# Products whose results nobody reads, in TensorE's pauses of a four-stage transformer pass

## The reference

```python
x = x + attn_a(layernorm(x), w_qkv, b_qkv)      # local: 16 heads of 16, softmax over groups of 32 tokens
x = x + ffn(layernorm(x), cn_*, gc_*, adaptive_range)
x = x + attn_b(layernorm(x), Wq, Wk, Wv, Wo, lambda_*, subln_g)
x = x + ffn(layernorm(x), cn_*, gc_*, adaptive_range)

# ffn: a gate of four small layers (256, 128, 64, 1), used three times
for _ in range(3):
    tf = sigmoid(gelu(gelu(gelu(out @ w1 + b1) @ w2 + b2) @ w3 + b3) @ w4 + b4)
    coupling = 0.1 + adaptive_range * (0.7 * gf + 0.3 * tf - 0.5) * 2.0
    out = out + coupling * twist(out)
# attn_b: differential attention over all 1024 tokens: 32 score maps with heads of 8,
# w = softmax(even map) - lam * softmax(odd map), values of width 16, RMS norm per head, then Wo
```

## Time and profile before

| | |
|---|---|
| Time, median of 3 runs | 8156.35 us (8153.01 to 8161.66) |
| Profiled execution, own time | 8150.33 us |
| Its span, first to last instruction | 8145.2 us |
| Busy: PE, DVE, ACT, POOL | 7508.5, 6885.6, 6208.0, 3537.0 us (92, 85, 76, 43%) |
| Mean granted TensorE clock | 0.959 |
| DMA | 297.66 MB, 37 GB/s in the mean |

### The profile page before, as it was taken

The page is one execution under the profiler, slowest core; times in us unless marked ns, Lnnn a source line. Parts: engine busy times, 40 slices in busy tenths (PEclk is TensorE's granted clock), DMA queues, the critical chain, the costliest instruction groups (busy, mean ns, idle before and its releaser), DMA issues. The chain is left out here.

```text
span 8145.2 us, 163210 instructions
## 1 busy us (share of the span) xinstructions
PE 7508.5 (92%) x64448; PEld 2698.0 (33%) x64448; DVE 6885.6 (85%) x8962; ACT 6208.0 (76%) x11230; POOL 3537.0 (43%) x4675
## 2 busy tenths in 40 slices
PE   6899988999889998899988999889998899989999
PEld 4322343223432234322343223432234322343223
DVE  5799768997689976899768997689976999669996
ACT  3599755997569975699756997569975699656996
POOL 4256233652336623355233662345513456134661
PEclk9899988999899998999998999999999999999999
DMA  0121101221012200121001210022200222002210
GB/s 31 48 47 44 29 12 49 47 47 24 12 54 44 47 23 12 55 47 44 21 12 56 47 44 22 9 58 46 48 21 7 62 43 48 23 4 63 45 44 25
DMA packets 591392, 297.66 MB, mean 37 GB/s; under 512 B 477238, under 2 KB 515638, under 8 KB 590582
## 3 DMA queue, kind: packets, MB, share of 16 engines
q1 hardware_dynamic: 590588, 286.82, 14.5%
HBM read 123.83 MB, written 67.37 MB: 23 GB/s over the span
## 5 line engine op out<-in xcount | busy, mean ns | idle before, releaser
L1459 DVE TENSOR_REDUCE mall<-ps 128x1 f32<-128x1024 f32 x4096 | 4662.3, 1212 | 80.7 <-PE ps L1396 80.0
L1544 ACT ACTIVATE work<-ps 128x512 f32<-128x512 f32 x8192 | 4335.7, 598 | 177.9 <-PE ps L1411 33.6
L1425 PE MATMUL ps<-work,vbuf 128*32 128x256 f32 x32768 | 2620.7, 392 | 58.6 <-ACT hh L1550 58.6
L1396 PE MATMUL ps<-kop,qop 48*128 48x512 bf16 x8192 | 2521.0, 386 | 46.8 <-DVE mall L1459 25.9
L1411 PE MATMUL ps<-qop,kop 51*128 51x512 bf16 x8192 | 2511.7, 384 | 24.6 <-DMA qop<-mT 13.7
L1425 PEld LDWEIGHTS ps<-work,vbuf 128*32 128x32 f32 x32768 | 654.0, 108 | 1727.8 <-issue 1001.7
L1411 PEld LDWEIGHTS ps<-qop,kop 51*128 51x128 bf16 x8192 | 512.9, 93 | 1783.4 <-ACT work L1544 1657.5
L1484 POOL TENSOR_TENSOR mall<-mall 128x16 f32<-128x16 f32 x512 | 113.9, 222 | 1772.8 <-DVE mall L1459 1752.8
L251 POOL TENSOR_TENSOR rstd<-rstd,nhalf 128x8 f32<-128x8 f32 x64 | 109.3, 1708 | 1637.8 <-DVE rstd L245 1637.8
L443 POOL TENSOR_TENSOR hh<-work,hmask 128x1024 f32<-128x1024 f32 x256 | 521.2, 2064 | 452.2 <-POOLq L1648 331.1
L1510 POOL TENSOR_TENSOR work<-work,none 128x16 f32<-128x16 f32 x224 | 650.6, 2904 | 18.2
(11 more groups left out here) (179 smaller groups left out, 8666.0 us busy)
## 6 DMA issues: line engine op xcount, KB each, us to landing
qop<-scratch SPq DMA_DIRECT2D x512, 64.0 KB
scratch<-work SPq DMA_DIRECT2D x32, 768.0 KB, 4.2
scratch<-hh SPq DMA_DIRECT2D x32, 768.0 KB, 3.6
kop<-scratch SPq DMA_DIRECT2D x256, 96.0 KB
vbuf<-in_x SPq DMA_DIRECT2D x9, 2048.0 KB, 8.3
qop<-scratch SPq DMA_DIRECT2D x512, 32.0 KB
kop<-scratch SPq DMA_DIRECT2D x256, 64.0 KB
out<-x SPq DMA_DIRECT2D x64, 256.0 KB, 2.1
```

The costliest lines, as they stand in the source:

```text
L1396: pe.matmul(ps[:, b + n, :], qop[r:r + KQ, s, i, t * P:(t + 1) * P], kop[r:r + KQ, s, i, half(n)], start=True, stop=True).then_inc(s_ms, 1)
L1425: mm = pe.matmul(ps[VW * i:VW * (i + 1), OB, cols], vp[:, b, t, (G * gl + i) // 2, :], prob[:, u % PS, i, cols], start=t == 0 and part == ...
L1459: v.tensor_reduce(mall[:, m // CUT % 2, to, col:col + 1], ps[:, b:b + NB, :].rearrange("p b n -> p (b n)"), AX.X, ALU.max).then_inc(s_mr, 1)
L1544: act.activation(prob[:, u % PS, hl, :], ps[:, EB[slot % len(EB)], :], ACT.Exp, scale=scale).then_inc(s_ex, 1)
```

## The change

A helper `busy` is added, which issues products of the identity with the first half of w1 into a named PSUM bank. Each has 128 rows, 128 columns of weights and 256 moving columns in f32. Nobody reads them, they wait for nothing, and they signal nothing. It is called at six places of TensorE's list, and no other engine's list is touched:

```diff
+        def busy(pe, bank, count):
+            for _ in range(count):
+                pe.matmul(ps[:, bank, 0:D], ident[:, :], w1[:, 0, :], start=True, stop=True)
...
                 def _(pe):                                   # layernorm: n2, n3, n4
+                    busy(pe, 7, 4)
                     for t in range(4 * N0, TT):
                         norm_turned(pe, t, s_h, s_tp)
...
+                    busy(pe, 7, 5)                           # local_attention
                     for t in range(TT + 2):
                         if t < TT:
                             scores(t)
...
                     layers(2, A)                             # ffn: f1, f2
+                    busy(pe, 5, 3)
                     layers(1, Z)
...
+                    busy(pe, 5, 4)
                     layers(2, Z)
...
                     project_pe(pe)                           # diff_attention
+                    busy(pe, 2, 6)
                     for e in CLOCK:
                         if value_tile(e) is not None:
                             project_values(pe, value_tile(e))
```

## The result

The changed kernel takes 8166.27 us (median of 20 runs, 8154.54 to 8170.11), the kernel before 8149.72 (20 runs beside them, 8131.49 to 8177.26). The ratio is 1.0019, with a 95% interval of 1.0011 to 1.0027: slower by 0.2%, where 0.2% faster was forecast. The profiled execution's span is 8162.3 us against 8145.2, and the mean granted clock is 0.972 against 0.959. TensorE's clock is full more often, and the kernel is slower.

The account below looks back on a forecast made before the run. VectorE's row of 512 maxima was taken to set the main block's length. Terms summed to -0.75 us a pass, -6.0 for eight, -6.7 once: -12.7, perhaps 2 more; from the median 8156.35 about 8141 us, range 8108 to 8178.

Parts of the forecast that it names:

- the same: Whole kernel: a time from 8140 to 8172.7 us, within 0.2% of no change; chance 0.42.
- Step 1: Local attention's start: five products bring the full clock sooner, and later work gains one for one; -2.6 us a pass.
- early end: Local attention: full clock 3.4 us after dense work starts, at 2093.7; the 16 records end at 2098.9, -2.5 us.
- Step 2: Layer norm n2: four products delay VectorE's first copy, 2.1 us at half clock, 0 at full; +1.3 us a pass taken.
- Step 3: Layer norm n3: four products take 1.72 us in a pause of 3.41 and change nothing; 0.
- Step 5: Feed-forwards f1 and f2: products in the pauses raise the clock for layer 2; -0.4 us in f1, -0.7 in f2.
- Step 6: Differential attention: six products delay the first maxima by 1.55 us a pass, nothing gives it back; pass 1 gains 6.7 once.
- Pass 1's 34.37 us: First L1396 to first L1411 in pass 1, against 27.64 in pass 3; dense products should prevent it, -6.7 us once.
- the clock stays up: Rival, chance 0.24: added products keep the clock full across pauses; -4.15 us a pass, 8116 us.
- A wash: Rival, chance 0.20: local attention's gain only 1.7 us, n2 pays 2.1; +1.45 us a pass, 8161 us.

Follow-up runs that it names:

- la_only: Only the change's five products at the start of local attention, added to the kernel before: 8109.62 us, ratio 0.9944 to the kernel before.
- la_end: la_only with two more products at each pass's end: 8109.78 us, ratio 0.9941 to the kernel before.
- da_only: Only the change's six products in front of the first maximum, added to the kernel before: 8153.53 us, ratio 0.9997 to the kernel before.
- full_shift: The whole change plus twelve short products of 64 columns in the pause in front of n3's turning: 8147.80 us, ratio 0.9986 to the kernel before.
- before_again: The kernel before, unchanged, run once more on a third chip: 8158.68 us, ratio 1.0004.
- la_end_shift: la_end plus twelve short products of 64 columns in the pause in front of n3's turning: 8164.70 us, ratio 1.0005 to the kernel before.
- la_end_n3_da: la_end plus n3's four products and the six in front of the first maximum: 8125.25 us, ratio 0.9966 to the kernel before.
- la_end_n3: la_end plus the four products in front of n3's turning: 8140.82 us, ratio 0.9990 to the kernel before.
- la_again: la_only, unchanged, run once more on a third chip: 8112.39 us, ratio 0.9954 to the kernel before.
- la_end_pad: la_end plus ten short products of 64 columns behind its last two at the pass's end: 8152.89 us, ratio 1.0004 to the kernel before.

## Why the prediction was wrong

The range (8108 to 8178) holds the result. The sign is wrong. By its own bounds (0.2% for a change) the result counts as the same, which had 0.42. By the prediction's steps:

- **Step 1, local attention: right at its own place, wrong for the block.** The early end came (-2.33, with 8.82 us for the first L360 records in pass 3, forecast 8.6). What failed is that such a gain "goes through to the later work one for one". More low time, 3.4 to 6.8 us, stands later in the same block in five passes, and 1.42 us are lost again behind the first L351. I had counted on low stretches that drop out, but they move. And I took the state at the pass's start as given: with a full clock there the gain is 4.5 us (la_only, la_end), and the change had one such pass in eight.
- **Step 2, n2: right**, at its upper end: +2.16 us in seven passes of eight and 0 in pass 1, +1.88 in the mean (forecast +1.3, bound 2.1).
- **Step 3, n3: wrong.** I gave 0, because VectorE sets the pace. The stretch around n3 got shorter by 1.52. Alone it is no gain, since the clock then falls on the first maxima, a price I had not looked for.
- **Step 5, the feed-forward: f1 right (-0.38), f2 wrong.** Its records have the full clock as forecast, but ScalarE holds the second half (1.45 us of waiting), and in three passes a low stretch begins with f2's first products. f2 took +0.64, where -0.7 was forecast.
- **Step 6, in front of the first maximum: delay right, price too high.** 1.82 us in the mean, but "nothing gives it back" is refuted by da_only (0.9997). Beside the second profile of the kernel before, 0.9 comes from VectorE's waits around the first exponentials, which a later start shortens, and 0.8 from late waits that are gone (the table below). Pass 1's 34.37 us are gone as forecast (26.3 in every pass). But in the second profile of the kernel before pass 1 takes 27.5 too, so the stretch belongs to one execution, and that the change took it away isn't shown.
- **The term that makes most of the loss was missing.** The sum has no term for late waits, since I had costed an added matmul by its time on TensorE alone. The row of maxima costs 2.46 a pass (forecast 0.71), and 1.39 of it are late waits, 2.18 us against 0.79. Without them the sum of the table would be +0.76 instead of +2.15; that this is still no gain comes from steps 1, 2 and 5. They come with the place of the program's own instructions: with 26 more matmuls ahead of the maxima a q8 packet falls into the transfer mT<-mall in half groups 4, 6, 8, 10 and 12. With that moved away (full_shift) the ratio is 0.9986, which on the forecast's median of 8156.35 is 8145 us; forecast were 8141. That they come so close is partly luck, since local attention, f2 and n3 missed by 1.7, 1.3 and -1.5 us a pass, and full_shift had a full clock in f2 besides.

The row of maxima by parts, us a pass in the mean of the eight passes; "early" are VectorE's waits up to 20 us behind the first exponential's scores:

| profile | ScalarE's last copy to first maximum | early waits | late waits | the maxima themselves |
|---|---|---|---|---|
| before | 1.65 | 4.50 | 0.79 | 582.8 |
| before_again | 1.85 | 3.74 | 0.83 | 582.8 |
| da_only | 3.48 | 2.88 | 0.01 | 582.8 |
| the change | 3.48 | 3.24 | 2.18 | 583.3 |
| full_shift | 3.48 | 2.46 | 0.00 | 582.8 |

Shown is that the number of matmuls ahead of the maxima moves the late half groups and with them some 2 us of waits a pass, in both directions (2.2 gone in full_shift, 1.9 brought in la_end_shift); and that a late transfer goes with a q8 packet and its moment. That the packet itself holds the transfer up is the reading that fits all traces; no run moved it without adding instructions. The Trainium skill ("Runtime: NRT & Kernel Launch", Instruction fetch mechanics) says that an engine fetches blocks of 16 KiB with 256 instructions through a DMA queue of its own, and that the cost of crossing one is mostly hidden. The traces agree with the block (519 packets of q8 with 8.50 MB, 16.4 KB each), and what the crossing costs TensorE itself no run here shows; the transfer beside it doesn't stay as it was. By an estimate from that page's figure, the 519 packets hold 132,864 instructions, and TensorE's rows have 2 x 65040 = 130,080, which fits q8 as TensorE's queue. By another estimate from that page's figure, a half group's 192 matmuls (8192 + 8192 + 32768 rows of scores and values in 256 half groups), each with its weight load, are 384 instructions or 1.5 blocks. That would make every second half group alike, as the traces show.

Of the rivals, "the clock stays up" (8116) didn't come: the mean clock did rise, and time was lost, so a raised clock alone says nothing. "A wash" (8161) is the nearest in time, but by luck: it had n2 at its upper end, and neither the late waits nor the gain around n3.

Open is what decides whether a pass begins at the full clock. It was 8 of 8 in la_end_n3_da and la_end_n3, 6 in la_only and 4 in la_again, which are one kernel, 4 in la_end, 1 in the change and in la_end_pad. I found no rule for it that holds in all the traces, and no run set it alone.

## What to carry to other kernels

- Products that nobody reads pay where the engine enters a block at the half clock and others wait for its first results: kernels with five of them at the head of local attention are faster by 0.5 to 0.6% here (la_only, la_again, and la_end with 0.9941; the two more of la_end can't be told apart), more than any larger set. About 0.1% of that is the kernel before's own late waits (0.8 us a pass), which five matmuls happen to move away. Fill one place at a time and keep what wins; the groups don't add, since a low stretch that is pushed out of one place comes back in the next.
- An added instruction has a place in the program as well as a time. In a loop it shifts the points at which instructions are loaded, and if a small transfer with little slack stands on the critical chain, look at whether that transfer's time changes in a fixed pattern. A dozen cheap instructions ahead of it are a test, and can be a cure.
- Where a leading engine runs ahead and then waits, a later start costs less than its delay (here about half came back from such waits). Read every single-group gain with the profile's parts beside it: some of it may lie in another block.

## What the hardware showed that I had not expected

- The transfer mT<-mall (one transpose) takes 2.4 us, and 3.0 to 4.5 when a 16 KB instruction packet begins 0.5 to 2.2 us behind its issue. Up to some 3.5 us it costs nothing here, and from there on it delays the next scores one for one (4.1 us: 0.6 later).
- The late half groups move by about 1.5 for each matmul added ahead of them (26 at 12 added, 4 at 26), between 9 and 26 added.
- A low stretch that is removed comes back elsewhere: around n3 it gave 0.7 to 1.5 us and cost 5.65 among the first maxima (593.12 against 587.47 us).
- The mean granted clock rose from 0.959 to 0.972 and the kernel got slower. la_end, the fastest, has 0.962.
